# A vision tower in one kernel: fewer and moved waits in four stages, and the last two experts taken by halves of the tokens

## What is computed

```python
h = tokens(x)                                        # 768 -> 256
h = h + attn0(layernorm(h))     # rmsnorm, global latent attention, + rmsnorm, local attention; 16 heads, 4 kv heads
h = h + moe(layernorm(h))       # 32 experts, top 8 of 2 groups of 4, plus 2 shared ones; silu(g) * u, inner 128
h = h + attn1(layernorm(h))     # 16 heads, softmax over 37 keys
h = h + ffn(layernorm(h))       # w1, gelu, w2 at width 1024; activations and weights rounded to 255 levels
                                # (x/scale rounded) @ (w/scale rounded).T + b, all times both scales
```

## Time and profile before

| what | value |
|---|---|
| median of 3 runs | 360.65 us (360.07 to 361.62) |
| the profiled execution | 360.19 us, of which the trace spans 358.4 us |
| PE busy | 341.2 us, 95% |
| DVE busy | 232.6 us, 65% |
| ACT busy | 196.9 us, 55% |
| POOL busy | 137.6 us, 38% |
| granted TensorE clock, mean | 0.999 |

### The profile page before, as it was taken

How to read it: one execution, slowest core, us unless ns; L and a number is a source line. 1 busy time by engine, 2 the same in 40 slices (tenths; PEclk the granted TensorE clock), 3 DMA queues, 4 the chain that set the end, 5 groups by cost and what they waited for, 6 DMA issues and landing times.

```text
span 358.4 us, 9932 instructions
## 1 busy us (share of the span) xinstructions
PE 341.2 (95%) x3931; PEld 292.8 (82%) x3931; DVE 232.6 (65%) x520; ACT 196.9 (55%) x400; POOL 137.6 (38%) x145
## 2 busy tenths in 40 slices
PE   8999889998988999999999999999999999999994
PEld 6866667676667989999999999999999678776662
DVE  3656788787879375555555555556557565666687
ACT  5367944787484335444444544544543786346772
POOL 0045761383160266555566544444440004241000
PEclk9999999999999999999999999999999999999999
DMA  8940000000560344455444445443410000000001
GB/s 284 405 159 1 3 5 7 24 3 5 171 182 3 96 115 137 145 156 155 138 122 148 137 154 155 137 135 136 143 27 2 0 0 4 6 4 3 2 0 68
DMA packets 14865, 32.08 MB, mean 90 GB/s; under 512 B 2480, under 2 KB 4464, under 8 KB 14576
## 3 DMA queue, kind: packets, MB, share of 16 engines
q1 hardware_dynamic: 13328, 30.48, 26.8%
q10 hardware_dynamic: 1504, 1.13, 0.9%
HBM read 30.91 MB, written 0.69 MB: 88 GB/s over the span
## 4 chain that ended last, share of the span: by engine, by line
PE 75%; DVE 10%; ACT 8%; issue 2%; DMA 1%; ACTq 1%; SPq 1%; POOL 1%; DVEq 0%
PE psum L1277 75%; DMA km<-in_experts 1%; DVE xn L907 1%; ACT region L861 1%; DVE nt L902 1%; ACTq L568 1%; DVE nt L904 1%; SPq L395 1%; ACT L589 1%; DVE km L1203 1%; ACT ah L746 1%; ACT region L681 1%; ACT e L693 1%; ACT sq L598 1%; DVE rt L1132 1%
## 5 line engine op out<-in xcount | busy, mean ns | idle before, releaser
L1277 PE MATMUL psum<-xh,split_all 128*128 128x296 f32 x544 | 121.5, 298 | 0.0
L506 POOL TENSOR_TENSOR split_all<-km,split_all 128x768 fp32r<-128x768 f32 x34 | 62.5, 1842 | 79.9 <-ACT split_all L725 79.9
L1277 PEld LDWEIGHTS psum<-xh,split_all 128*128 128x128 f32 x544 | 91.4, 188 | 0.1
L1277 PE MATMUL psum<-xl,split_all 128*128 128x296 f32 (+1 forms) x288 | 85.5, 301 | 0.3 <-POOL xl L549 0.3
L746 ACT ACTIVATE ah<-rt 128x296 fp32r<-128x296 f32 x64 | 28.9, 452 | 72.7 <-DVE rt L1132 66.0
L1277 PEld LDWEIGHTS psum<-xl,split_all 128*128 128x128 f32 (+1 forms) x288 | 53.3, 187 | 1.5 <-issue 1.1
L1277 PE MATMUL psum<-ah,split_all 128*128 128x296 f32 x272 | 48.5, 300 | 1.7 <-ACT ah L746 1.6
L1134 DVE TENSOR_TENSOR al<-rt,ah 128x296 fp32r<-128x296 f32 x60 | 28.0, 467 | 31.1 <-ACT ah L746 31.1
L1129 DVE TENSOR_TENSOR rb<-psum,wb 128x296 f32<-128x296 f32 x60 | 28.0, 467 | 24.4 <-ACT psum L744 24.4
L1277 PEld LDWEIGHTS psum<-ah,split_all 128*128 128x128 f32 x272 | 40.5, 189 | 2.6 <-ACT ah L746 2.1
L1132 DVE TENSOR_TENSOR rt<-rb,psum 128x296 f32<-128x296 f32 x60 | 27.8, 463 | 4.8
(11 more groups left out here) (225 smaller groups left out, 582.0 us busy)
## 6 DMA issues: line engine op xcount, KB each, us to landing
km<-in_experts SPq DMA_DIRECT2D x34, 384.0 KB, 4.0
wb<-weights SPq DMA_DIRECT2D x32, 296.0 KB, 3.6
w_sb<-in_w SPq DMA_DIRECT2D x2, 1024.0 KB, 8.6
region<-in_x SPq DMA_DIRECT2D x6, 296.0 KB, 4.9
region<-in_w_lin ACTq DMA_DIRECT2D x6, 128.0 KB, 5.6
qkv_sb<-in_qkv_w SPq DMA_DIRECT2D x1, 768.0 KB, 4.9
cst<-in_consts SPq DMA_DIRECT2D x1, 502.5 KB, 7.0
out<-x SPq DMA_DIRECT2D x2, 148.0 KB, 1.8
```

The source lines that it names most:

```text
L506: nc.gpsimd.tensor_tensor(wl[i], ring[i], wh[i].bitcast(f32), ALU.subtract)\
L1277: return nc.tensor.matmul(out_, lhsT, rhs, start=start, stop=stop, skip_group_check=True)
```

## The change

Seven edits, each within its own stage; the count of experts, matmul shapes in the loop and transfers stay.

1. In `qk_units` of both attentions DVE, not ACT, copies the first half's values, between its part of unit 4 and of unit 5 (`first_values_copied`, semaphore `s_v0`); its two key variants of the second half move from behind unit 4 to the end. The banks of `grouped_values` are swapped (`1 - p % 2`), so its first pair waits for five units, and the third for the sixth.
2. Between the attentions `stream_variance(1)` goes ahead of the projection of unit 1 on PE, and `stream_rsqrt(1)` ahead of unit 1's copy on ACT.
3. In the router comparisons are joined in one tile (`ahead`), three small steps fall out, the weights' scales are worked out after the router, and the shared products stand at earlier places, between a step and the wait on it.
4. The last four half-units go in the order (32, 0), (33, 0), (32, 1), (33, 1). Half 0 of the stream is copied, averaged and centred beside half 1's sums; the table of the reciprocal root is loaded before the last rounding; `s_acc` and its matmul are gone.
5. In the last attention the seeds go between the last `weighted_values`, and the second half's projection is made in quarters of 148 columns, the first once six of the eight pairs are normalised.
6. `b2` is seeded into the four banks by `ident` (four matmuls of 296 columns) in the place of 16 of the 18 matmuls that keep PE at work; the sum of stream and projection is made by POOL, per half, as soon as the projection is copied; the two steps L1260 and L1263 on DVE are gone.
7. Names, counts of semaphores and the bank of one `peaks_spread` follow.

```diff
@@ attention, ACT and DVE and PE @@
+                    if a == 1 and u == 1:
+                        stream_rsqrt(1)
...
                 load_table(ACT.Exp)
-                act_e.wait_ge(s_vz, 1)
-                values_copied(a, 0)
                 attention(a)
...
+                    if u == NPROJ:
+                        first_values_copied(a)
...
-                    if u >= 2 and QK_UNITS[u - 2][0] == 2:
+                    if u in (QK_UNITS.index((2, 0)) + 2, NPROJ):
...
-                bank = ps[p % 2]
+                bank = ps[1 - p % 2]
...
+                    if a == 1 and u == 0:
+                        stream_variance(1)
                     if u + 1 < NPROJ:
                         projection(a, u + 1)
...
-                            pe.wait_ge(s_v, 2 * a + 1)
+                            pe.wait_ge(s_v0, a + 1)
+                            pe.wait_ge(s_qk, NPROJ * (a + 1) - 1)
+                        if p == 2:
                             pe.wait_ge(s_qk, NPROJ * (a + 1))
@@ router, DVE @@
-            link(ins)
+            own[0] += 1
+            ins.then_inc(s_dve, 1)
+            shared_product(0, 0)
+            dve.wait_ge(s_dve, own[0])
...
-            shared_product(0, 0)
             link(nc.vector.tensor_scalar(masked[:], masked[:], 0.0, None, ALU.add))
...
+            shared_product(2, 0)
+            dve.wait_ge(s_dve, own[0])
@@ the last half-units, ACT @@
+            for n in range(2 * UNITS - 4, 2 * UNITS - 1):
+                expert_unit(n, n % 2, ps[6 + n % 2][:, 0:HALF])
...
+            experts_copied(0)
+            silu(2 * UNITS - 1, ps[7][:, 0:HALF], 4)
+            load_table(ACT.Abs_reciprocal_sqrt)
+            rounded(2 * UNITS - 1)
+            last_squares(0)
+            experts_copied(1)
+            rsqrt_of_half(0)
+            last_squares(1)
+            rsqrt_of_half(1)
@@ the last half-units, DVE (N = 64) @@
+            gate_weighted(N + 2, 0, ps[6][:, 0:HALF], row_of(N + 2))
+            up_product(N + 2, 0)
+            experts_copied(0)
+            product_low_part(N + 2, 0)
+            gate_weighted(N + 3, 1, ps[7][:, 0:HALF], row_of(N + 3))
+            up_product(N + 3, 1)
+            centred_chunk(0, 0)
+            product_low_part(N + 3, 1)
+            centred_chunk(0, 1)
+            experts_copied(1)
+            for c in range(C):
+                centred_chunk(1, c)
             norm_apply(3, 8)
@@ the last half-units, PE @@
+            for n in range(2 * UNITS - 4, 2 * UNITS):
+                if n + 1 < 2 * UNITS:
+                    u, hf = LAST_UNITS[n + 1]
+                    up_sums(u, u % NRING, hf, 4, n + 1)
+                if n == 2 * UNITS - 2:
+                    last_mean(0)
+                u, hf = LAST_UNITS[n]
+                down_sums(u, u % NRING, hf, False, n)
+            keep_busy(7, 2)
+            last_variance(0)
+            last_mean(1)
+            keep_busy(7, 6)
+            last_variance(1)
+            keep_busy(7, 6)
@@ end of the last attention, PE @@
+                seed_projection(1)
+                pe.wait_ge(s_on, 3 * PAIRS - 2)
+                add_projection(0, 0)
                 pe.wait_ge(s_sq, 2 * C + 1)
...
-                keep_busy(7, 3)
+                add_projection(1, 0)
                 pe.wait_ge(s_on, 3 * PAIRS)
                 for m in range(C):
-                    centred_projection(1, m, True)
+                    add_projection(m, 1)
@@ end of the last feed-forward block @@
+            for hf in range(2):
+                pool.wait_ge(s_hn, hf + 1)
+                nc.gpsimd.tensor_tensor(x0[:, :, half(hf)], x0[:, :, half(hf)], h[:, :, half(hf)], ALU.add).then_inc(s_xh0, 1)
...
-            keep_busy(0, 18)
+            for m in range(C):
+                for hf in range(2):
+                    mm(ps[2 * m + hf][:, 0:HALF], const("ident"), vector("b2")[:, m:m + 1].broadcast_to([P, HALF]), True, False)
+            keep_busy(5, 2)
...
-            link(nc.vector.tensor_scalar(b2s[:], vector("b2"), sxw[:, 1:2], None, ALU.mult))
-            dve.wait_ge(s_hn, 2)
-            for m in range(C):
-                ins = nc.vector.scalar_tensor_tensor(x0[:, m, :], x0[:, m, :], b2s[:, m:m + 1], h[:, m, :],
-                                                     ALU.add, ALU.add)
-            link(ins)
             for hf in range(2):
+                dve.wait_ge(s_xh0, hf + 1)
                 dve.wait_ge(s_f2, hf + 1)
```

213 lines of the change are left out of this document (125 added, 88 removed).

## The result

Four executions of the changed kernel beside four of the kernel before, on one chip: median 354.77 us (353.91 to 357.04) against 361.02 us (360.07 to 361.62), a ratio of 0.985, 95% interval 0.982 to 0.988. The forecast was 354.1, range 352.2 to 357.0. Two later series, each beside the kernel before on a chip of its own, gave the changed kernel 357.2 (ratio 0.989, 0.983 to 0.995) and 355.2 (0.985, 0.979 to 0.991); over all twelve executions the median is 355.3 and the spread 353.2 to 359.5.

What follows compares the result with a forecast made beforehand. The prediction took PE to bound the kernel, three quarters of the chain of waits, with short DVE and ACT hand-overs. Seven terms summed to 6.3 us off the profiled 360.19, giving 354.1 us, range 352.2 to 357.0.

Steps and rivals of the forecast that it cites:

- Terms 1 to 3: First attention 0.8 us, between attentions 0.95, second attention 0.7: DVE copies values, variance goes ahead of a projection, PE starts earlier.
- Term 4: Router: PE's 1.16 us stop goes, but the fourth silu behind two ACT stores limits the gain; 0.8 us.
- Term 5: Last experts and norm: half 0 normalised beside half 1's sums, last sums 0.7 later, first q and k products 1.35 us earlier.
- Term 6: End of last attention: half the projection's columns move ahead of the last pair's wait, second bank's square earlier; 0.65 us.
- Term 7: End of kernel: two DVE steps before the last products and a small scaling go, seeds replace fillers; 1.05 us.
- the page's figure of 2.66 for a switch: Last experts' table load: with the skill page's load plus drain, that term would be 0.1 and the total 355.1 us.
- the clock falls: Rival: less filler at 278 to 285 us lowers PE's clock to 1.2 GHz; 362.3 us, chance 0.04 shared with another stage.
- the prediction's own last sentence: Whole kernel: forecast wrong if DVE's copy exceeds 1.5 us, last rounding starts over 1.5 behind table load, or clock under 0.9.
- The other two signs: Signs of a wrong forecast: DVE's copy over 1.5 us; last rounding starting over 1.5 us behind the table load's start.

Runs made afterwards that it cites:

- e5: Changed kernel with the first values of each attention copied again by ScalarE behind its table load; one execution, 356.31 us.
- e6: Changed kernel with the last norm's first mean on PE ahead of the first quarter of the projection's sums; one execution, 356.34 us.
- e7: Changed kernel with the last experts' edit taken back: old half-unit order, both halves normalised at the end; 357.24 us, ratio 0.992 to the kernel before.
- e2: The kernel before, unchanged, run and profiled again; 361.26 us.
- e3: Changed kernel with 14 more filler matmuls between mean and variance of the second norm; 357.07 us beside 357.20 for the changed kernel.
- e11: The changed kernel, unchanged, run a third time; 355.18 us.
- e1: The changed kernel, unchanged, run a second time; 357.20 us.
- e8: Changed kernel with two ScalarE roundings behind the first two silus, two GpSimd low parts later, fourth silu ahead of ScalarE's stores; 361.27 us, ratio 1.001 to kernel before.
- e9: As e8, but third low part on VectorE and SyncE's seventh and eighth expert transfers behind the stores of the routing weights; 353.85 us, ratio 0.981 to kernel before.
- e10: Changed kernel with 23 instead of 19 filler matmuls ahead of the first product; 355.54 us beside 355.18 for the changed kernel.
- e4: Changed kernel with two of ScalarE's four expert-weight roundings moved behind the second norm and GpSimd's fourth low part later; 356.87 us beside 357.20 for the changed kernel.

## Why the prediction was right, point by point

**The terms.** Against the earlier trace rows, from the profiled execution of the changed kernel and, where a fall or a wait hides one, from the runs above:

| term | forecast | measured | from |
|---|---|---|---|
| 1 to 3, attentions and between | 2.45 | 2.35 | stage table, row 2: 89.31 less 86.96 |
| 4, router | 0.8 | 0.7 | row 4: 30.78 less 30.05 (e5) or 30.11 (e6) |
| 5, last experts | 1.35 | 1.68 | e7 |
| 6, end of last attention | 0.65 | 0.43 | row 6, 0.33 of it behind the last reciprocal |
| 7, end | 1.05 | 0.95 | row 7 |
| sum | 6.3 | 6.1 | |

Each measured value is a difference of single profiles. Row 2 was 86.65 to 87.84 in the nine profiles with this code of the attentions and without a late rise of the clock, and 89.31 and 89.78 before, so terms 1 to 3 are 1.5 to 3.1 by the pair that one takes. And the sum isn't yet the gain: the prediction let the loop's pace stay as it was and had no term for the second norm's transfer or for a fall. The pace took 0.93 back, which leaves 5.2. Over all three series the medians are 5.1 apart (355.3 and 360.4). Of the recorded sums, the upper bounds add up to 8.7 and not 8.6, and a matmul of 296 columns is 2.17/4 = 0.54 us and not 0.51; neither moves a term by much more than 0.1.

**Terms 1 to 3** came as drawn in the order of events, with sizes off inside, and with the copy's share smaller than drawn (e5):

```profile
42.49 0.47 PE L1355 MATMUL psum<-e,region 101*32 101x74 f32 x16
43.92 1.06 DVE L1017 RECIPROCAL rc<-psum 128x148 f32<-128x148 f32 x1
50.42 0.59 PE L1355 MATMUL psum<-qt,km 64*37 64x74 f32 x24 [0.78 <-issue]
64.35 0.53 DVE L929 SCALAR_TENSOR_TENSOR nt<-psum,eps,nt 128x296 f32<-128x296 f32 x1 [0.85 <-ACT nt L622]
79.86 0.46 PE L1355 MATMUL psum<-e,region 101*32 101x74 f32 x16
81.23 1.07 DVE L1017 RECIPROCAL rc<-psum 128x148 f32<-128x148 f32 x1
89.20 0.61 PE L1355 MATMUL psum<-qt,km 64*37 64x74 f32 x25 [0.70 <-issue]
```

PE's idle of 1.07 is gone, and VectorE's before the norm's third step is 0.85 for 1.84. Counted stage by stage it was 0.94, 0.96 and 0.45, for 0.8, 0.95 and 0.7. VectorE's copy took 1.38 us for the 1.2 taken. In the second attention VectorE came 0.55 earlier, but PE stopped 0.70 us for instructions at 89.20 where it had stopped for 0.17: I had counted on PE's stop "for instructions" in the first attention only, but in the second it comes and goes with the execution (e2, the kernel before, has 0.92 us there; from first to last reciprocal the second attention took 10.70 to 11.33 us over all profiles, and 10.73 and 11.33 in the two of the kernel before).

**Term 4** had its mechanism right. The stop of 1.16 us is gone, and PE's lead is held up by the fourth silu behind the two stores, as said. The lines: the stores, 1.61 us and not the 1.34 of before, and the new idle.

```profile
117.64 1.61 ACTq L369 DMA_DIRECT2D weights<-wtr  x2
119.30 0.42 ACT L750 ACTIVATE ra<-psum 128x296 f32<-128x296 f32 x1 [2.25 <-issue]
120.75 0.81 PE L1355 MATMUL psum<-ah,split_all 128*128 128x296 f32 x4 [0.58 <-ACT ah L752]
```

**Term 5**: these are the rows that it named. The changed kernel was 0.31 us ahead at the loop's end (266.55 for 266.86 us), which is to be added to each.

```profile
276.67 1.28 ACT L595 ACT_TABLE_LOAD   x1
278.07 0.43 ACT L769 ACTIVATE ah<-rt 128x296 fp32r<-128x296 f32 x1
278.54 0.47 DVE L1188 TENSOR_TENSOR al<-rt,ah 128x296 fp32r<-128x296 f32 x1 [0.26 <-ACT ah L769]
282.71 0.52 DVE L929 SCALAR_TENSOR_TENSOR nt<-psum,eps,nt 128x296 f32<-128x296 f32 x1
284.82 0.41 PE L1355 MATMUL psum<-xn,qkv_sb 128*128 128x296 f32 x1
```

The rounding begins 1.40 us behind the table load's start, as in the earlier trace rows: the page's figure of 2.66 for a switch (the Trainium skill, ScalarE: Activation LUTs, "What ACT_TABLE_LOAD costs"), by which the sum would have been 355.1, doesn't show here either. With the 0.31 the low part is 0.6 late for 0.7 forecast, the correction begins at 283.02 for 283.4, and the q products at 285.13 for 285.3 to 285.4. Every hand-over is 0.1 to 0.4 earlier than drawn and none is out of order, which fits the 0.3 by which the term was too small. The clock was 1.00 throughout: the stage that I had feared for the fall was not the one.

**Term 6** was the weakest: 0.43 of 0.65, and e3, with the same end, has 48.39 in row 6 where the changed kernel has 47.97, which is no gain against 48.40. The quarter now ahead of the mean makes the mean late as said, but the gain doesn't hang on that (e6): PE is at work without a gap, and what was saved can be the three fillers (0.54 us at most). I had costed an order of waits where the bound was PE's own work.

**Term 7**: VectorE's last steps begin at 350.94, as the last products end (346.66 + 4.38 = 351.04, half 0 a little before), where before they began 0.9 behind. GpSimd's sum took 1.44 us for each half and ended over 13 us ahead of its use; the four seeds (eight records) took the fillers' place, in 2.17 us for 2.06 forecast.

```profile
331.98 1.44 POOL L560 TENSOR_TENSOR x<-x,h 128x592 f32<-128x592 f32 x1 [8.72 <-ACT x L855]
344.40 2.17 PE L1355 MATMUL psum<-vec,cst 128*128 128x296 f32 x8
346.66 4.38 PE L1355 MATMUL psum<-km,w2q 128*128 128x296 bf16 x32
350.94 1.39 DVE L1347 SCALAR_TENSOR_TENSOR x<-psum,sxw,x 128x296 f32<-128x296 f32 x3 [0.81 <-PE psum L1355]
```

**What it missed.** The prediction took no row of the second norm, whose squares stand on ScalarE behind four roundings that wait for a transfer. The trace of before had it (its last three roundings began 1.24 us late for that transfer), but I read the chain of waits' small share of transfers as "hardly any". The wait doesn't cut off what the attentions gain, since the transfers are issued behind their last scores: the issue came 2.0 us earlier in the first pair of profiles, and the squares 1.1 (94.19 for 95.31 behind the first split; e6, e7 and e11 have 94.02, 93.72 and 92.49, before again 96.39). But it adds a length of its own that differs by the execution, 8.4 to 9.4 us from issue to squares in the changed kernel's profiles and 8.5 and 8.8 before. It cost 0 to 1.9 us (row 3 less 5.34), against 0.7 to 1.3 before.

And of the clock I named the wrong place. The rival "the clock falls" had its lower level and its sign right and its size far off, because I priced it with eight us of work behind it; a fall in the changed kernel lasted 3.4 us and cost 0.9 to 1.7. By the prediction's own last sentence, a granted clock under 0.9 anywhere makes the forecast wrong: all three profiles of the changed kernel show one (0.61 and 0.52 in the first, 0.50 in e1 and e11). The other two signs stayed away: the copy took 1.38 us, under 1.5, and the last rounding began 1.40 behind the table load.

So most terms and their order were right, and that the time came out so close, 354.77 for 354.1, is in part luck. It rests on three executions of the first series with a mean clock of 1.00 (353.9 to 355.2), of which there is no trace; all three profiles of the changed kernel are longer (356.0 to 359.5), and e5 and e6, without a fall, took 356.3. In the second series the median, 357.2, lay just outside the range.

## What to carry to other kernels

When several hand-overs in a row are shortened, look between them for one stage that is released by something not in that row, here a transfer whose start hangs on a buffer of the stage before. Its start moves with the stage before, but its length doesn't shrink and differs by a us from one execution to the next, so price that stage from the issue on. Moving a step means walking through every in-order queue that waits for it, SyncE's too, and asking which VectorE operations with two SBUF inputs will run beside a moved GpSimd one; of the orders that removed the same wait, the first gained nothing, the second lost 6 us and the last gained 1.7 (medians, across chips). Where PE has no idle, price work taken from PE, not waits taken from others.

## What the hardware showed that I had not expected

- The granted clock fell to the lower level in all three profiles of the changed kernel and in four of its nine variants' (e7, e8 twice, e9, e10), always from a point between 100 and 127 us, for 3.4 us each time but one (6.8 in e8), and in neither of the kernel before. A fall came behind an idle of 1.72 us, behind one of 1.80, and inside one of 5.47, but five of the eight came where the last idle was 0.33 to 0.61 (e8's first, e1, e10, e11, e7); idles of 0.99, 0.91 and 1.09 (e5, e6, e4) brought none. What decides it stays open.
- One loop, two paces: 2.433 or 2.450 us for a half-unit of 18 matmuls, at clock 1.00 and without idle, nothing between, in 14 profiles. Both profiles of the kernel before, e4 and e10 have the first, the changed kernel's three and seven variants the second. e4 has the changed kernel's very PE program and only another order on ScalarE and GpSimd; e3 and e10 both shift PE's program and came out differently. In the four fast ones PE reached its upper clock 5.9 to 6.7 us after the start, in the ten slow ones outside that. It is worth 0.9 us; I have no cause that is shown.
- From the issue of four transfers of 384 KB to the end of ScalarE's fourth rounding it took 8.5, 9.4 and 9.5 us in the three profiles of the changed kernel, the same program on the same buffers.
- The same 19 fillers don't always bring the clock up in time: once it took 10.1 us, and 1.6 us were gone by 11 us.
